# Decoder layer with routed experts on one core: sixteen row buffers, one staging pass, padded combine weights, expert numbers in eights, pair sums on PE

## What is computed

```python
aff = sigmoid(x @ wa)                       # 16 experts
topk_p, topk_i = top_k(aff, 2)
topk_p = topk_p / sum(topk_p)
combine = sum(one_hot(topk_i, 16) * topk_p)
expert(x) = (gelu(x @ g + gb) * (x @ w1 + b1)) @ w2 + b2     # 256 -> 128 -> 256
x = layernorm(x + sum of 2 shared experts + sum over 16 routed experts of combine * expert(x))
```

## Time and profile before

| | |
|---|---|
| median of 3 runs | 774.76 us (771.25 to 776.35) |
| the profiled execution | 777.45 us, its span 775.6 us |
| busy in the span | PE 522.6 us (67%), DVE 449.6 (58%), POOL 362.6 (47%), ACT 276.7 (36%) |
| share of the chain that ended last | PE 42%, DVE 21%, issue 12%, DMA 8%, POOL 7%, ACT 5% |

### The profile page before, as it was taken

The page is one execution under the profiler, slowest core; times in us unless marked ns, Lnnn a source line. Parts: engine busy times, 40 slices in busy tenths (PEclk is TensorE's granted clock), DMA queues, the critical chain, the costliest instruction groups (busy, mean ns, idle before and its releaser), DMA issues.

```text
span 775.6 us, 13954 instructions
## 1 busy us (share of the span) xinstructions
PE 522.6 (67%) x4116; PEld 310.2 (40%) x4116; DVE 449.6 (58%) x869; ACT 276.7 (36%) x642; POOL 362.6 (47%) x405
## 2 busy tenths in 40 slices
PE   6798857883000188887755878859889788878800
PEld 3343322221000167776512435535344466656600
DVE  1875659993898025647434797993831134444536
ACT  2476465340000033334243655654421023333314
POOL 1361129770797022424368998800167213343453
PEclk9899977775555597889777998988969889999965
DMA  9970001237001711211000000083022303343363
GB/s 298 302 124 0 0 1 61 101 116 128 1 0 13 150 43 52 71 41 48 1 8 0 11 10 7 7 332 151 0 86 102 101 24 111 114 127 99 113 236 122
DMA packets 61588, 64.23 MB, mean 83 GB/s; under 512 B 25434, under 2 KB 53100, under 8 KB 61420
## 3 DMA queue, kind: packets, MB, share of 16 engines
q1 hardware_dynamic: 57707, 52.98, 23.8%
q0 software_dynamic: 3840, 10.75, 3.8%
HBM read 36.27 MB, written 27.44 MB: 82 GB/s over the span
## 4 chain that ended last, share of the span: by engine, by line
PE 42%; DVE 21%; issue 12%; DMA 8%; POOL 7%; ACT 5%; SPq 2%; DVEq 1%; ACTq 0%; POOLq 0%
DVE work L1432 4%; PE ps L738 4%; PE ps L651 3%; PE ps L825 3%; PE ps L978 3%; PE ps L992 3%; DVE work L298 3%; DVE arena L301 3%; PE ps L1037 3%; POOL arena L1957 3%; PE ps L641 2%; DMA rows_dr<-work 2%; DMA work<-slots_dr 2%; PE ps L879 2%; PE ps L789 2%
## 5 line engine op out<-in xcount | busy, mean ns | idle before, releaser
L2003 POOL DMA_INDIRECT rows_dr<-work x48 | 46.0, 958 | 88.8 <-DVE work L1782 74.7
L759 PE MATMUL ps<-xT 32*32 32x64 f32 x768 | 15.0, 227 | 89.3 <-DMA xT<-inverse_dr 87.3
L1432 DVE SCALAR_TENSOR_TENSOR work<-ps,colp,work 96x504 f32<-96x504 f32 (+5 forms) x84 | 59.6, 729 | 22.8 <-ACT work L1088 20.8
L1957 POOL TENSOR_TENSOR arena<-work,consts 128x1024 f32<-128x1024 f32 x32 | 64.1, 2033 | 15.8 <-ACT work L1245 15.8
L1037 PE MATMUL ps<-vsg,work 128*128 x192 | 54.7, 409 | 10.1 <-ACT work L1366 7.4
L1768 DVE TENSOR_TENSOR work<-ps,front 128x256 f32<-128x256 f32 x48 | 20.4, 425 | 58.7 <-PE ps L1037 58.2
L651 PE MATMUL ps<-xT,front 128*96 128x512 f32 (+3 forms) x112 | 50.5, 595 | 0.0
L759 PEld LDWEIGHTS ps<-xT 32*32 32x32 f32 x768 | 12.8, 113 | 91.4 <-issue 90.5
L1923 POOL TENSOR_TENSOR work<-work 128x384 f32<-128x384 f32 x16 | 13.2, 849 | 75.3 <-DVE work L1563 75.3
L1037 PEld LDWEIGHTS ps<-vsg,work 128*128 128x128 f32 x192 | 33.8, 196 | 19.9 <-issue 16.5
L1996 POOL DMA_INDIRECT slots_dr<-work,slots_i x32 | 31.0, 969 | 19.6 <-issue 10.8
(11 more groups left out here) (230 smaller groups left out, 1354.0 us busy)
## 6 DMA issues: line engine op xcount, KB each, us to landing
slots_dr<-zero SPq DMA_DIRECT2D x24, 272.0 KB, 4.0
work<-slots_dr SPq DMA_DIRECT2D x48, 136.0 KB
vsg<-wexp_dram SPq DMA_DIRECT2D x4, 1536.0 KB, 18.4
vsg<-rows_dr SPq DMA_DIRECT2D x4, 1024.0 KB, 8.8
scores_dr<-work SPq DMA_DIRECT2D x16, 192.0 KB, 1.9
attend_dr<-work SPq DMA_DIRECT2D x16, 192.0 KB, 2.0
xT<-scores_dr SPq DMA_DIRECT2D x16, 192.0 KB, 3.9
xT<-attend_dr SPq DMA_DIRECT2D x8, 384.0 KB, 3.3
```

The lines of the kernel that those rows point to most:

```text
L1432: dve.scalar_tensor_tensor(y[:, :, d:T], z[:, :, 0:T - d], taps[0:r, j, KSZ - 1 - d:KSZ - d], y[:, :, d:T], ALU.mult, ALU.add).then_inc(s_ ...
L1957: ins = pool.tensor_tensor(kblk[:, u, f], over(kqT[:, u, 0, f, :], 1, 8), over(consts[:, C_KM:C_KM + 8], 2, P), ALU.mult)
L2003: pool.indirect_dma_start(out=rows_dr, out_offset=bass.IndirectOffsetOnAxis(ap=xg[:, j % XG, S_DEST:S_DEST + 1].bitcast(U32), axis=0), in_ ...
```

## The change

1. `xst` holds all 16 tiles (32 rows of 272 values in each partition). `stage_rows` waits for no scatter any more and its last two calls come one gelu pair earlier; POOL writes all destinations and weights in two instructions and issues the 32 scatters behind one wait a group.
2. The combine weights of a tile are padded with zeros from 18 to 128 columns (`comb_flat` in `work`, cleared by POOL), `combT` and `b2s` have 128 rows, and L1010 and L990 become 128 by 128 blocks. The shared weights, `combT` and `b2s` move to `front`, and `b1r` to `xT`, so its broadcast is issued only when the last `shared_hidden` has read `xT`.
3. XG goes from 8 to 16, with eight semaphores (XS): the load of slot j waits for the load of slot j - 8 and the output of slot j - 16. The outputs keep eight buffers (YO).
4. PE and DVE load eight expert numbers at once, without a check of their bounds, before slot 0 and then ahead of each eighth slot.
5. The pair sum in the tail becomes two products of PE with the identity, added in PSUM, for each tile; DVE adds the PSUM bank to the token. The tail's pieces are two tiles (GC 2) in place of four.

```diff
-XG, YO, GC = 8, 8, 4
+XG, XS, YO, GC, RB = 16, 8, 8, 2, 8
...
-        b1r = front[:, 0:E * 2 * F]
+        b1r = xT[:, 0:E * 2 * F]
...
-        wsh = work[:, 7768:7768 + SH * EW].rearrange("p (u c) -> p u c", u=SH)
+        wsh = front[:, 0:SH * EW].rearrange("p (u c) -> p u c", u=SH)
...
-        combT = work[0:NE, 4608:4608 + NTOK]
-        b2s = work[0:NE, 6656:6656 + D]
+        combT = front[:, SH * EW:SH * EW + NTOK]
+        b2s = front[:, SH * EW + NTOK:SH * EW + NTOK + D]
...
-        comb_flat = arena[:, 7364:7364 + NT * NE]
-        comb = comb_flat.rearrange("p (n e) -> p n e", e=NE)
+        comb_flat = work[:, 8704:8704 + NT * P]
+        comb = comb_flat.rearrange("p (n e) -> p n e", e=P)
         comb2 = arena[:, 7652:7652 + NT * E].rearrange("p (n e) -> p n e", e=E)
...
-        xst = work[:, 0:2 * 4 * 2 * SW].rearrange("p (b t k c) -> p b t k c", b=2, t=4, k=2)
...
+        xst = work[:, 0:NT * 2 * SW].rearrange("p (n k c) -> p n k c", n=NT, k=2)
...
+        s_xg = [dma_sem(f"slot_rows_then_expert_rows_in{v}") for v in range(XS)]
...
+        s_got = s_xg
...
+            sp.wait_ge(s_pw, at(2))
+            sp.dma_start(b2s[0:NE, :], b2_d).then_inc(s_rw, 16)
             for e in range(0, E, 4):
                 sp.dma_start(wres[:, e * EW:(e + 4) * EW].rearrange("p (e c) -> p e c", e=4),
                              wexp_d[e:e + 4].rearrange("e p c -> p e c")).then_inc(s_wr, 16)
+            sp.wait_ge(s_h, at(SH * NG))
+            sp.dma_start(b1r, b1_d.partition_broadcast(P)).then_inc(s_rw, 16)
             for b in range(2):
                 sp.wait_ge(s_scat[b], 16 * NT)
             def load_rows(j):
-                v = j % XG
+                if j >= XS:
+                    sp.wait_ge(s_xg[j % XS], 16 * (j // XS))
                 if j >= XG:
-                    sp.wait_ge(s_yout[v], 16 * (j // XG))
-                sp.dma_start(xg[:, v, :], slots_dr[j * P:(j + 1) * P]).then_inc(s_xg[v], 16)
+                    sp.wait_ge(s_yout[j % YO], 16 * ((j - XG) // YO + 1))
+                sp.dma_start(xg[:, j % XG, :], slots_dr[j * P:(j + 1) * P]).then_inc(s_xg[j % XS], 16)
...
-            pe.wait_ge(s_cmb, at(4))
+            pe.wait_ge(s_cmb, at(5))
             for g in range(NG):
                 for t in range(SPG):
                     n = SPG * g + t
-                    mm = pe.transpose(ps[0:NE, 4 + g, t * P:(t + 1) * P], comb_flat[:, n * NE:(n + 1) * NE], ident)
+                    mm = pe.transpose(ps[:, 4 + g, t * P:(t + 1) * P], comb_flat[:, n * P:(n + 1) * P], ident)
                 mm.then_inc(s_lgt, 1)
...
-                pe.wait_ge(s_xg[j % XG], 16 * (j // XG + 1))
+                pe.wait_ge(s_xg[j % XS], 16 * (j // XS + 1))
...
-            def hidden(j):
-                e = pe.value_load(expert_i[0:1, j:j + 1], min_val=0, max_val=(E - 1) * EW)
+            def hidden(j, e):
                 pe.wait_ge(s_xge, at(j + 1))
...
+            def next_experts(j):
+                _, found = nc.values_load_multi_w_load_instructions(
+                    expert_i[0:1, j:j + RB], engines=[mybir.EngineType.PE], min_val=0, max_val=(E - 1) * EW,
+                    skip_runtime_bounds_check_because="the routing clamps the expert's number to E - 1")
+                which.update(zip(range(j, j + RB), found))
+            next_experts(0)
...
+                if (j + 2) % RB == 0 and j + 2 < NSLOT:
+                    next_experts(j + 2)
+            for n in range(NT):
+                if n % GC == 0:
+                    pe.wait_ge(s_got[n // GC], 16 * (NSLOT // XS + 1))
+                pe.wait_ge(s_yoe, at(NSLOT))
+                if n >= 8:
+                    pe.wait_ge(s_f1, at(n - 7))
+                for k in range(2):
+                    mm = pe.matmul(ps[:, n % 8, 0:D], ident, got[:, n, k, :], start=(k == 0), stop=(k == 1))
+                mm.then_inc(s_yo, 1)
...
             def stage_rows(m):
-                if m >= 2:
-                    act.wait_ge(s_scat[m % 2], 128 * (m // 2))
-                act.activation(xst[:, m % 2, :, :, 0:D], over(x3[:, 4 * m:4 * m + 4, :], 2, 2), ACT.Copy).then_inc(s_xst, 1)
+                act.activation(xst[:, 4 * m:4 * m + 4, :, 0:D], over(x3[:, 4 * m:4 * m + 4, :], 2, 2), ACT.Copy).then_inc(s_xst, 1)
...
-                if 1 <= g < NG - 1:
-                    stage_rows(g + 1)
+                if g < NG - 2:
+                    stage_rows(g + 2)
...
+            def next_biases(j):
+                _, found = nc.values_load_multi_w_load_instructions(
+                    bias_i[0:1, j:j + RB], engines=[mybir.EngineType.DVE], min_val=0, max_val=(E - 1) * D,
+                    skip_runtime_bounds_check_because="the routing clamps the expert's number to E - 1")
+                rows_of.update(zip(range(j, j + RB), found))
...
-                e = dve.value_load(bias_i[0:1, j:j + 1], min_val=0, max_val=(E - 1) * D)
+                e = rows_of[j]
...
+                if (j + 1) % RB == 0 and j + 1 < NSLOT:
+                    next_biases(j + 1)
...
-                dve.wait_ge(s_cmb, at(4 + n + 1))
-                dve.tensor_tensor(x3[:, n, :], x3[:, n, :], got[:, n, 0, :], ALU.add).then_inc(s_f1, 1)
+                dve.wait_ge(s_yo, at(NSLOT + n + 1))
+                dve.tensor_tensor(x3[:, n, :], x3[:, n, :], ps[:, n % 8, 0:D], ALU.add).then_inc(s_f1, 1)
...
-            pool.wait_ge(s_xr2, at(NT))
+            pool.memset(comb_flat, 0.0).then_inc(s_cmb, 1)
+            pool.wait_ge(s_cmb, at(1))
             pool.memset(comb[:, :, E:NE], 1.0).then_inc(s_cmb, 1)
+            pool.wait_ge(s_x2, at(NT))
+            pool.tensor_copy(xst[:, :, :, S_DEST].bitcast(U32), destc).then_inc(s_ix, 1)
             pool.wait_ge(s_mask, at(3))
+            pool.tensor_copy(xst[:, :, :, S_WEIGHT], w_flat.rearrange("p (k n) -> p n k", k=2)).then_inc(s_ix, 1)
             pool.tensor_tensor(comb[:, :, 0:E], pick, over(best[:, 5], 2, E), ALU.mult).then_inc(s_cmb, 1)
             pool.tensor_tensor(comb2, pick2, over(best[:, 6], 2, E), ALU.mult).then_inc(s_cmb, 1)
-            pool.wait_ge(s_cmb, at(3))
+            pool.wait_ge(s_cmb, at(4))
             pool.tensor_tensor(comb[:, :, 0:E], comb[:, :, 0:E], comb2, ALU.add).then_inc(s_cmb, 1)
-            pool.wait_ge(s_x2, at(NT))
-            weights = w_flat.rearrange("p (k n) -> p n k", k=2)
-            def tag_rows(m):
-                n = slice(4 * m, 4 * m + 4)
-                pool.tensor_copy(xst[:, m % 2, :, :, S_DEST].bitcast(U32), destc[:, n, :]).then_inc(s_ix, 1)
-                pool.tensor_copy(xst[:, m % 2, :, :, S_WEIGHT], weights[:, n, :]).then_inc(s_ix, 1)
+            pool.wait_ge(s_slots, at(2))
+            pool.wait_ge(s_zero_in, 8 * NSLOT + 16)
+            pool.wait_ge(s_ix, at(2))
...
             for m in range(NT // 4):
-                if m >= 2:
-                    pool.wait_ge(s_scat[m % 2], 128 * (m // 2))
-                tag_rows(m)
-                if m == 0:
-                    pool.wait_ge(s_slots, at(2))
-                    pool.wait_ge(s_zero_in, 8 * NSLOT + 16)
                 pool.wait_ge(s_xst, at(m + 1))
-                pool.wait_ge(s_ix, at(2 * m + 2))
                 alone(pool)
-                for t in range(4):
+                for n in range(4 * m, 4 * m + 4):
                     for k in range(2):
-                        c = 2 * (4 * m + t) + k
+                        c = 2 * n + k
                         pool.indirect_dma_start(
                             out=slots_dr, out_offset=bass.IndirectOffsetOnAxis(ap=slots_i[:, c:c + 1], axis=0),
-                            in_=xst[:, m % 2, t, k, :], in_offset=None).then_inc(s_scat[m % 2], 16)
+                            in_=xst[:, n, k, :], in_offset=None).then_inc(s_scat[m % 2], 16)
...
-            for n in range(NT):
-                if n % GC == 0:
-                    pool.wait_ge(s_got[n // GC], 32)
-                pool.tensor_tensor(got[:, n, 0, :], got[:, n, 0, :], got[:, n, 1, :], ALU.add).then_inc(s_cmb, 1)
```

36 lines of the change are left out of this document (17 added, 19 removed).

## The result

The changed kernel takes 722.3 us (median of four runs, 717.3 to 731.8) against 773.0 us of the kernel before on the same chip (766.2 to 776.4): a ratio of 0.933, interval 0.924 to 0.943. The profiled execution took 723.59 us with a span of 721.6; the span before was 775.6.

What follows compares the result with a forecast made beforehand. PE was taken to bound the shared stage, the row-buffer ring's DMA path the slots, POOL and DVE the tail. Terms -6 (shared), -28 + 4.5 (slots), -1 (tail) gave -30.5: span 745.1, forecast 744 us, range 733 to 761.

Steps and rivals of the forecast that it cites:

- The ring: Slot loop: 16 row buffers take the DMA path out of each turn, leaving 1.65 us a slot; -28 us.
- Numbers in eights: Slot loop: single loads are hidden, while each load of eight costs 0.9 us, five in the loop; +4.5 us.
- The rival of eights in series: Slot loop: PE's and DVE's loads of eight follow one another and drain the pipeline; +15.1 us, 788 us, chance 0.03.
- Padding: Shared outputs: the 18-row product, 0.62 us, takes 0.53 as a full block, over 16 tiles; -1.4 us.
- the -6 of the shared stage: Shared experts: half of a gain between 0 and 11 us, mainly from shorter low-clock stretches; -6 us.
- The clock: Shared experts: full blocks shorten half-clock stretches, 12.0 us together; a low stretch is likelier shortened than absent.
- The floor under the shared stage: End of shared experts: rows not there before about 614.5 against 625, so at most 11 us gained.
- the three tag pairs: Token staging: removing them saves POOL about 2 us, hidden behind PE, so nothing.
- Tail: After the slots: pieces of two tiles start PE earlier and pair sums move to PE; -1 us taken.
- My own sum with a slow start: Tail: PE starts slowly, then runs at full clock; 3.6 + 17.0 + 2.5 + 6.1 = 29.2 us, so -2.3.
- The move of the sums to PE: Tail: two products a tile take 1.06 us at full clock, 2.01 at half, against POOL's 0.80.

Runs made afterwards that it cites:

- b_pad: The kernel before with one edit, combine weights as full blocks of 128 rows; ratio 0.994 to the kernel before.
- a_rows18: The changed kernel with the bias product of the shared outputs over 18 rows again; median 748.4 us, no ratio on record.
- b_ring16: The kernel before with 16 row buffers and nothing else; ratio 0.975 to the kernel before.
- b_ring16e: The kernel before with 16 row buffers and expert numbers loaded in eights; ratio 0.970 to the kernel before.
- a_same3: The changed kernel unaltered, measured again as a control; median 743.1 us, ratio 0.955 to the kernel before.
- a_gc4: The changed kernel with tail pieces of four tiles instead of two, pair sums kept on PE; ratio 0.964 to the kernel before.
- a_twoprod2: The changed kernel with two sets of shared-stage product buffers and DVE's next products ahead of its additions, second run; 734.6 us, ratio 0.941 to the kernel before.
- a_twobuf: The changed kernel with tokens staged in two buffers and four pairs of tags again; ratio 0.949 to the kernel before.
- a_again: The changed kernel unaltered, measured once more; median 739.1 us, ratio 0.956 to the kernel before.
- a_poolpairs: The changed kernel with pair sums back on POOL, pieces of two tiles kept; median 746.6 us, ratio 0.961 to the kernel before.
- e_hold: The changed kernel with POOL's token scatters held back until the shared outputs are done; ratio 0.992 to the kernel before.

## Why the prediction was wrong

The sum was -30.5 us of span and the measured change -54.0. Of the 23.5 us between them, 12.3 lie in the shared stage, 7.9 in the slots and 3.3 in the tail; the steps that failed are the size of the padding, half a clock term under a floor that was set too late, the sign of the eights, and the price of a pair sum.

**The ring: right.** The mechanism, the bound that takes its place (PE, 1.62 us a slot without a gap) and the size were as forecast: -28 expected for the ring with single loads hidden. The runs split it otherwise: -25.8 for the ring in the kernel before, and 5.9 more that only eights give. In the changed kernel, with eights, the ring is worth 19.5.

**Numbers in eights: the first wrong step.** "So nothing is saved in the steady state" and +4.5 for five loads. I costed the eight from above, one round trip and eight register operations ahead of what needs them, and the single loads at nothing because they were hidden in slots held up by the ring. Both halves fell: an eight takes 0.59 us and delays nothing, since PE has work queued; single loads cost 5.9 to 7.2 us over 48 slots, 0.12 to 0.15 each, once PE is the bound. The sign was wrong: instead of -28 + 4.5 the slots gave -31.4. The trace of the kernel before held a hint: behind single loads many hidden products took 1.0 to 1.14 us instead of 0.86. The rival of eights in series is refuted with it.
**Padding: the second.** The term was 16 x 0.09 = -1.4 us and went into the -6 of the shared stage without being named there. It came from a product of 0.62 us that should become 0.53. It became 0.43, and the unaltered L995 behind it fell from 1.06 to 0.86: 16 x 0.38 = 6.1 us, shown by b_pad and undone by a_rows18. My step took the row of L992 as the full-height price, where that row stood behind an 18-row product and held some of its cost. The same row mis-priced the pair sums of the tail.

**The clock: right mechanism, half its size taken.** I counted 12.0 us of cold stretches and took about half. In the recorded profile all are gone, and they were 11.0 us: 3.4 in the first group, 2.4 in the hidden group, 5.2 in the last up to its last product. PE's stage then adds up: 3.6 us earlier start, which no run explains, 6.1 for the tiles, 11.0 for the clock and 2.1 for the shorter wait ahead of the last group (3.91 to 1.83 us, the late notices of the kernel before) are the 22.7 us by which the last product moved, within 0.1. That full blocks bring the clock back and the 18-row mixture does not is shown in both directions: cold for all four tiles with 18 rows (kernel before, a_rows18, b_ring16, b_ring16e), at full clock after 3 to 5 us of work with full blocks (b_pad, a_same3, a_gc4, a_twoprod2), and never cold there behind the same 1.83 us of rest. The Trainium skill (TensorE: Matmul & The Clock Gate, Part 1: The HAM clock gate) says that sustained activity releases the half clock; PE was busy 12.34 of 13 us in a_rows18 at a mean clock of 0.53, so the trace contradicts the sentence here, as it did at 614 to 625 us of the kernel before.

**The floor under the shared stage: the third.** I let it gain 11 us at most, since rows could not be there before 614.5. They came at 607.3: the first scatter started 2.0 us earlier, the three tag pairs gone saved 2.1 (2.5 in a_twobuf), which I had booked as hidden behind PE, and from the last scatter's start to the rows passed 4.6 us instead of the 7.7 I had worked out. The 7.7 were a wrong reading: in the kernel before SP issues the first load of slot rows at 609.29, only 2.5 us behind the last scatter's start, and such a load took 2.08 us after the change, so rows could have been there at about 611.4.
```profile
609.29 3.67 SPq L612 DMA_DIRECT2D work<-slots_dr  x8
```
Had I asked what is late once PE's stage shrinks, POOL's tag writes would have had their price.

**Tail: undersized.** -4.3 instead of -1, all of it from pieces of two tiles, which I had priced only by the earlier start. My own sum with a slow start, 3.6 + 17.0 + 2.5 + 6.1 = 29.2, was 2.0 us too long: 3.9 + 16.7 + 6.6 = 27.2 was measured, the slow start included in the 16.7, since a tile of pair sums takes 0.86 us at full clock and not 1.06. The move of the sums to PE, half of my working, is worth 0.3 us, within the noise: PE's 16.7 us with a cold start against POOL's 13.0, and DVE's additions fast again (0.33 us apart instead of 0.88 beside POOL).

**What no step had**: the kernel's own spread. The changed kernel, taken four times, gave ratios of 0.933, 0.956, 0.949 and 0.955, and medians of 722.3, 739.1, 729.2 and 743.1 us; its 18 runs lie between 717.3 and 746.2, with their middle at 733.9, just inside the range. By the mean of the last three ratios, 0.953, the kernel before at 774.8 becomes 739 us. That is no vindication but luck: a tile, a tail and a load term that were too small in gain and an unforeseen stall, which brings the slots' rows 13 to 16 us later behind the first scatter (a_same3, a_again), partly cancel.

## What to carry to other kernels

Price an operation's neighbours with it: the 18-row product cost more in the instructions behind it and in the clock than in its own duration. When a bound goes, go again through everything booked as hidden: single value loads, tag writes and DMA landings each had a price the moment the ring or PE's stage no longer covered them. Split a change by one-edit kernels from both ends (undo one in the new, do one in the old); where the two agree, as the 6.1 us of the padding do (undone in a_rows18, done in b_pad), the price can be trusted even if one stage wanders by 17 us between runs. Where they don't, as 25.8 and 19.5 us for the ring, the parts act on each other, and a split holds only for the order in which it was made.

## What the runs showed of the hardware

- PE's notices of finished products can be late by 11.5 us (a_same3), 17.2 (a_poolpairs) and, in a_twoprod2, 20.4, while POOL issues indirect scatters 1.27 us apart; several late ones then come 0.08 us behind one another (a_gc4, a_same3). The profile shows it as DVE waiting for "remote" and as an idle PE with "issue" as its reason. Where the lateness is small the label is PE's (kernel before), so the sure sign is an addition that starts well behind the end of its product. It was absent with the scatters held back (one profile) or 1.47 us apart (three).
- The stage ahead of the scatters moves by itself: the first token scatter starts at 560 to 565 us in most profiles and at 569.5 to 577.4 in six of them, of kernels that differ only behind it (e_hold apart, whose scatters are held back). In those six the mean granted clock from 400 to 450 us was 0.80 to 0.84, in the other profiles it was 0.88 to 0.90. What tips it stays open.
- A product over 18 rows of 128 is not cheaper than one over 128: 0.62 against 0.43 us for two instructions of 256 columns at the same granted clock.
